# Gathers of a graph network's edge stage read their indices in place

## What is computed

```python
def _L1_gnn_ref(h, rbf, edge_index, We1, be1, We2, be2, Wlin, Wn1, bn1, Wn2, bn2):
    src, dst = (edge_index[0], edge_index[1])
    w = silu(rbf @ We1 + be1) @ We2 + be2          # per edge, 200000 x 64 -> 128
    m = w * (h[src] @ Wlin)                        # row of the source node
    agg = segment_sum(m, dst, num_segments=h.shape[0])
    out = silu(agg @ Wn1 + bn1) @ Wn2 + bn2
    return h + out
```

## Time and profile before

| | |
|---|---|
| median of 3 runs | 4196.25 us (4185.68 to 4204.25) |
| profiled execution | 4190.64 us, span 4188.9 us |
| PE busy | 3078.5 us (73%) |
| DVE busy | 2098.1 us (50%) |
| POOL busy | 1449.0 us (35%), nearly all in the edge stage |
| ACT busy | 962.0 us (23%) |
| DMA | 325.5 MB, mean 78 GB/s; q1 (hardware queues) 15.9% of the DMA engines' time, q0 (GpSimd's) 8.9% |

### The profile page before, as it was taken

One profiled execution on the slowest core, in us unless ns is written; L12 is line 12 of the kernel. 1 busy time (PEld: TensorE's weight loads), 2 busy tenths in 40 slices (PEclk: granted clock), 3 DMA queues, 4 the chain that ended last, 5 costly groups with the idle time before them and its releaser, 6 DMA issues.

```text
span 4188.9 us, 82895 instructions
## 1 busy us (share of the span) xinstructions
PE 3078.5 (73%) x19882; PEld 2243.1 (54%) x19883; DVE 2098.1 (50%) x4806; ACT 962.0 (23%) x2058; POOL 1449.0 (35%) x1549
## 2 busy tenths in 40 slices
PE   6979999999979966666666666666666666666667
PEld 5623567777769954444444444444444444444445
DVE  8999999999984432333223332233322333323333
ACT  4101244566641111111111111111111111111111
POOL 0000000000000034555555555555555555555552
PEclk8989999999999977777777777777777777777778
DMA  1000111222237932222222222222222222222222
GB/s 52 0 0 32 47 78 78 109 109 109 109 155 298 344 121 57 59 57 59 59 60 59 57 59 60 60 59 57 59 60 60 59 59 58 59 60 59 57 57 58
DMA packets 289446, 325.50 MB, mean 78 GB/s; under 512 B 236303, under 2 KB 249640, under 8 KB 276606
## 3 DMA queue, kind: packets, MB, share of 16 engines
q1 hardware_dynamic: 234382, 218.90, 15.9%
q0 software_dynamic: 49504, 102.66, 8.9%
q10 hardware_dynamic: 5264, 1.36, 0.1%
HBM read 237.69 MB, written 85.09 MB: 77 GB/s over the span
## 4 chain that ended last, share of the span: by engine, by line
PE 40%; ACTq 26%; issue 25%; DVE 4%; ACT 3%; DVEq 1%; another core or an unknown queue 1%; DMA 0%; SPq 0%; POOL 0%; POOLq 0%
ACTq L390 20%; PE pa L1543 8%; PE pb L1395 7%; PE pa L1395 7%; PE pc L1389 5%; ACTq L386 5%; PE pd L1389 4%; PE pd L1353 2%; ACT shared L786 2%; PE pb L1554 1%; PE pf L1355 1%; PE pc L1571 1%; PE pb L1480 1%; DVE shared L1030 1%
## 5 line engine op out<-in xcount | busy, mean ns | idle before, releaser
L544 POOL DMA_INDIRECT shared<-lin_table,idx x1516 | 1434.1, 946 | 1183.0 <-ACT idx L666 542.3
L1543 PE MATMUL pa<-shared,we_sb 64*128 64x512 f32 x784 | 393.8, 1096 | 945.2 <-ACT shared L786 835.5
L1543 PEld LDWEIGHTS pa<-shared,we_sb 64*128 64x128 f32 x784 | 95.8, 296 | 984.8 <-ACT shared L786 869.4
L573 POOL DMA_DIRECT2D lin_table<-c x12 | 9.3, 772 | 1498.6 <-issue 1308.9
L1225 DVE TENSOR_TENSOR agg<-agg,pf 128x128 f32 x98 | 28.3, 289 | 891.0 <-remote 868.8
L1554 PE MATMUL pb<-we_sb,shared 128*128 128x128 f32 x3136 | 460.1, 290 | 6.6 <-issue 6.6
L1225 DVE TENSOR_TENSOR agg<-agg,pc 128x128 f32 x98 | 28.3, 289 | 855.5 <-remote 806.0
L1554 PEld LDWEIGHTS pb<-we_sb,shared 128*128 128x128 f32 x3136 | 384.5, 193 | 96.5 <-issue 96.0
L666 ACT ACTIVATE idx<-idx_all 128x8 int32 (+1 forms) x196 | 40.8, 210 | 1683.3 <-issue 1683.3
L1030 DVE TENSOR_SCALAR shared<-col_h,shared 128x784 bf16<-128x784 f16 x1092 | 408.9, 426 | 5.1 <-issue 4.3
L791 ACT ACTIVATE shared<-pa,be_col 128x512 f32<-128x512 f32 x392 | 248.3, 685 | 483.5 <-PE pa L1543 344.8
(11 more groups left out here) (238 smaller groups left out, 4286.9 us busy)
## 6 DMA issues: line engine op xcount, KB each, us to landing
adjacency<-shared SPq DMA_DIRECT2D x49, 1568.0 KB, 5.6
shared<-adjacency SPq DMA_DIRECT2D x49, 1568.0 KB, 8.7
table_sb<-lin_table SPq DMA_DIRECT2D x3384, 0.5 KB
shared<-in_edge_attr_dram SPq DMA_DIRECT2D x195, 256.0 KB
table_sb<-lin_table ACTq DMA_DIRECT2D x2632, 0.5 KB
shared<-lin_table,idx POOLq DMA_INDIRECT x1516
lin_table<-c POOLq DMA_DIRECT2D x12, 256.0 KB, 7.1
out_dram<-xr SPq DMA_DIRECT2D x12, 256.0 KB
```

The lines of the kernel that those rows point to most:

```text
L544: pool.indirect_dma_start(out=dest(s, j), out_offset=None, in_=table, in_offset=bass.IndirectOffsetOnAxis(ap=idx[:, s, j:j + 1], axis=0)). ...
L1543: pe.matmul(pa[:, h, :], we1_sb[half, :], ea_t[half, :], start=True, stop=True).then_inc(hid_mm, 1)
```

## The change

GpSimd's gathers in the edge stage take each tile's row numbers from its column of `idx_all` in place of the block `idx[s]`. The column's place is a constant in each instruction, so GpSimd's loop over turns is written out turn by turn. GpSimd no longer waits for `idx_ready` in this stage, and ScalarE no longer copies index blocks for it nor waits for landed gathers. The wait for `msg_ready` stays as it was. The two passes that are taken only when a test at run time asks for them keep `gather`, `idx` and the copies.

```diff
-            def linear_rows(s, j):
-                return gat[:, s, j, :]
+            def linear_gather(g, s, tiles=U):
+                for j in range(tiles):
+                    pool.indirect_dma_start(
+                        out=gat[:, s, j, :], out_offset=None, in_=lin_table,
+                        in_offset=bass.IndirectOffsetOnAxis(ap=idx_all[:, g * U + j:g * U + j + 1], axis=0)).then_inc(lin.gathered[s], 16)
 
             def gather_turn(it, tiles):
                 for s in range(RING):
-                    pool.wait_ge(lin.idx_ready, it * RING + (s + 1))
                     pool.wait_ge(msg_ready, (it * RING + (s - RING + 1)) * 2)
                     pool.sem_inc(passed, 1)
-                    gather(lin, lin_table, linear_rows, s, tiles if s == RING - 1 else U)
+                    linear_gather(it * RING + s, s, tiles if s == RING - 1 else U)
             for s in range(RING):
-                pool.wait_ge(lin.idx_ready, s + 1)
-                gather(lin, lin_table, linear_rows, s)
-            with pool.Fori(1, ITERS - 1) as it:
+                linear_gather(s, s)
+            for it in range(1, ITERS - 1):
                 gather_turn(it, ASIDE)
             gather_turn(ITERS - 1, LAST_TILES)
...
-            first_idx(lin)
             edge_act(0)
...
             def act_turn(it, par=None):
                 for s in range(RING):
                     edge_act(it * RING + (s + 1), None if par is None else (it + 1, par, s))
-                    after_gather(lin, it, s, 1 if s == RING - 1 else 0)
```

## The result

The changed kernel takes 4323.4 us, median of its five runs, against 4196.25 us. Two of the five lie near 4565 us and the others near 4320 us, and it is with the latter that the ratio is 1.029 (95% interval 1.027 to 1.031), slower. The profile read here is from a second set of runs of the same kernel (x1_after_again: execution 4325.2 us, span 4323.5 us, against a span of 4188.9 us before). The two spans differ by 134.6 us. The gather stands in a function of its own now, L582 for L544, and the code behind it has moved by a line: the sums' addition L1224 for L1225, the products L1207 and L1203 for L1208 and L1204, ScalarE's activation after a batch L787 for L786.

A forecast was written before the change was run, and what follows sets the result against it. The bound was taken as a loop through GpSimd, whose batches hold TensorE's results. 4190.6 us plus +0.93 us x 190 = +177 us, other terms taken as nothing, gave 4368 us; range 4150 to 4530 us.

The forecast's parts named there:

- from then on every batch needs the products that VectorE makes in this very gap: Edge stage: without the index wait, VectorE's products gate GpSimd's batches; +177 us, chance 0.60.
- hardly ever holds it now: GpSimd's msg_ready wait before a batch: seldom binding in the kernel before, since its products were made the previous turn.
- The early one: Gap between GpSimd's batches when VectorE already had its sums: 4.12 us, +0.08 us a batch, +15 us in all.
- a short gap gives less time and the next is long: Gaps between GpSimd's batches: short and long both occur, so the middle was taken, 4.97 us.
- The index copies: ScalarE's copies and wait for gathered: 32 us if ScalarE alone set the pace, nothing where products set the gap.
- The operand: GpSimd's gathers reading the table with longer rows: taken as 0, bounded by -0.01 to +0.08 us a gather.
- The loop written out: GpSimd's 47 turns written in a line: taken as 0, with 123 us either way as the bound.
- ScalarE's last row issue: Sign in the edge stage: it would come sooner after a batch's end than 2.3 us.
- (a): Rival: GpSimd runs pairs of batches end to end, -125 us, 4066 us; chance 0.14.
- (b): Rival: ScalarE's queue is the bound, so only its 0.17 us a group go, 4159 us; chance 0.12.
- (c): Rival: GpSimd without gaps starves ScalarE's row issues, +400 us, 4590 us; chance 0.09.
- that it ends with the batch is: TensorE's results reach VectorE only some 2 us after GpSimd's batch has ended, whether 8 or 7 gathers.

The follow-up runs named there:

- experiment 2: Changed kernel with GpSimd's wait for ScalarE's idx_ready signal put back, nothing copied; 4170.4 us, ratio 0.990 to the kernel before.
- experiment 9: Changed kernel with row transfers split evenly, 16 issues a group each on SyncE and ScalarE; 4239.7 us, ratio 1.020 to the kernel before.
- experiment 3: Kernel before with GpSimd's loop over turns written out and nothing else; 4194.6 us, ratio 0.997.
- experiment 5: Changed kernel with all eight tiles gathered by GpSimd and no row issues on ScalarE and SyncE; 4155.0 us, ratio 0.987 to the kernel before.
- experiment 4: Changed kernel with GpSimd also waiting for the second layer's matmuls of the group three before; 4297.9 us, ratio 1.021 to the kernel before.
- experiment 6: Changed kernel with four gathers a group, their rows used twice in the products; 3875.1 us, ratio 0.921 to the kernel before.
- experiment 7: Kernel of experiment 2 with one row transfer a group moved from ScalarE to SyncE (19 and 13 issues); 4432.2 us, ratio 1.053 to the kernel before.
- experiment 8: Kernel of experiment 4 with two row transfers a group moved from SyncE to ScalarE (16 and 16); 4065.1 us, ratio 0.965 to the kernel before.

## Why the prediction was right, and where it wasn't

**Direction and mechanism: right.** The step "from then on every batch needs the products that VectorE makes in this very gap" is in the waits: 175 gaps put down to L1207 and L1203, where before the index copy ended most. Experiment 2 settles it: the same gathers, the same indices, the wait back, and the loss is gone. Span and gaps agree (134.6 against 135 us). The 0.80 us from products to gather, which came from one place, holds: it is 0.80 or 0.81 us in all 165 gaps put down to products between 1700 and 4060 us.

This also settles what looked like a weak point. The prediction said that msg_ready "hardly ever holds it now", while the earlier trace rows puts 224.0 us of the gaps before down to L1208. In 49 of the 50 such gaps between 1700 and 4060 us the last product ended only 0.04 to 0.60 us before the gather, too late to have released it. One is in the earlier trace rows: the gather starts at 2536.78, before the products' end at 2537.33, and the index copy stands as far ahead of it as in the first of these gaps (0.88 and 0.89 us):

```profile
2535.69 0.21 ACT L666 ACTIVATE idx<-idx_all 128x8 int32 x1 [8.54 <-issue]
```

**The size: +135 us for the +177 forecast; the early end was mis-sized.** I took the middle of two gaps, 5.82 and 4.12 us. The late one measures 5.93 us, near the sum of rows that gave it. The early one measures 3.50 us, not 4.12: I had it from one place of the trace before, where the products ended 3.32 us after the batch, and in the changed kernel they end as little as 2.4 us after a batch of 7 gathers, where half of them is made while the batch still runs. With 3.50 the middle is 4.71 us, +0.67 us, +128 us. So the even mixture, which I had argued as "a short gap gives less time and the next is long", held almost exactly: 94 and 90, and the two kinds take turns. That it came out even is in part luck. The prediction's reason, the length of the gap before, doesn't force it: in experiment 9 the gaps are ended by products as well, and there short ones follow short ones. The sum also had no term for the split of the rows, on which 0.9 of the 2.9% hang.

**The index copies: right in size.** Forecast -32 us where they count, together with ScalarE's wait for landed gathers. They count nothing in the changed kernel, whose gaps end with products; where ScalarE's signal ends the gap (experiment 2 against 3) they bring some 28 us.

**The operand: nothing, as forecast.** The gathers' minimum, median and maximum are those of the earlier trace rows to the nanosecond.

**The loop written out: forecast 0, measured 0.3% faster.** The Trainium skill (Advanced Engine Details and Errata, ISA Cache) gives the size of the instruction cache, but no price of a refill and no word on loops; the estimate of +20 us for refills was worked out from it with a row of ScalarE. The runs don't bear the estimate out: experiment 3 is some 12 us faster, and the steps between gathers are the same 0.30 us.

**ScalarE's last row issue: not sooner than 2.3 us, but sooner than before.** The 2.3 us were those of one batch. The rows below give 2537.91, 2552.72 and 2566.45, which is 3.69, 2.55 and 2.49 us after the ends at 2534.22, 2550.17 and 2563.96. These are late ones: over the batches of 1700 to 4060 us the median is 2.36 us, against 2.64 us in the kernel before.

```profile
2530.69 7.22 ACTq L390 DMA_DIRECT2D table_sb<-lin_table  x14
...
2544.48 8.24 ACTq L390 DMA_DIRECT2D table_sb<-lin_table  x14
...
2557.47 8.98 ACTq L390 DMA_DIRECT2D table_sb<-lin_table  x14
```

So the sign as it was worded wasn't met, and the step behind it, that ScalarE's issues end sooner after a batch in a longer turn, holds weakly, by some 0.3 us. The chain that ended last still gives ScalarE's queue 26%, yet no gap is put down to it; whether the changed kernel would gain from fewer issues on ScalarE was not tried.

**The rivals.** (a), pairs of batches, appears in the changed kernel only at the stage's two ends; it appears in experiment 5, where no rows are issued, as the forecast's reason against it said, and there gives 13.4 us a group rather than 12.8. (b), ScalarE's queue as the only bound, fell: it would have made the changed kernel as fast as experiment 2. (c), ScalarE's issues starved, didn't come, but its likeness did in another place that I hadn't weighed: SyncE. In experiments 4, 6 and 7 it is SyncE's 18 or 19 issues that come too late: its queue has 40, 43 and 33% of their chains. The prediction read ScalarE's queue because the chain named it and left out the other one, which had 0% of the chain and almost no slack.

**What stays open.** That GpSimd's gathers hold TensorE's results is shown, since the hold-up ends earlier when the run of gathers is cut to half and stays when the row issues are gone; by what means they hold them isn't. Nor is the rule by which some get out: in the changed kernel the dividing line lies near 4.5 us into a batch (the latest that wasn't held was finished at 4.56 us, the earliest that was at 4.35 us), but in experiment 6 results finished 3.0 to 4.0 us into a batch were held while some finished at 3.3 to 3.5 us were not, and in experiment 9 seven in ten get out before the end (126 of 175 between 1700 and 4100 us), many after the sixth gather. The prediction's "that it ends with the batch is" (in the profile) holds in the changed kernel and nearly always in experiments 5 and 6. It fails in experiment 9, and it wasn't quite so in the kernel before either: there 13 of 140 sums finished during a batch of 8 got out 1.8 to 4.7 us later and yet before its end. The part of the split in the changed kernel's loss is known by experiment 9 alone, as 0.9% across two chips; a changed kernel with fewer rows on both engines was not run.

## What to carry to other kernels

When a wait is taken out, the next wait in line sets the release; find when that comes, from the trace, and whether the old wait kept the engine a step behind its buffers, so that the next one was always met. The moment of release can be worth more than the work: here a wait without any work, put where the second layer ends, together with an even split of row issues, gave 3.5%, and either alone was slower than the kernel before. And a queue that has 0% of the chain may have no slack: move one issue onto it and see, before something else is made faster.

## What the runs showed of the chip

A run of GpSimd's gathers mostly holds back TensorE's finished results from VectorE until after its last gather: by 1.3 us after a run of 4 (experiment 6), 2.0 us after 8 (the changed kernel) and 3.3 us after 16 (experiment 5, where the median wait is 14.9 us with no row transfers issued beside them; after its rarer runs of 8 the median is 3.5 us). In the changed kernel results that TensorE finishes early in a run aren't held (2544.94, added at 2545.08), and in experiment 9 most get out before its end.

Row issues on ScalarE and SyncE go more slowly beside those gathers. In the changed kernel (x1_after_again, pauses over 2.5 us left out) SyncE starts one every 0.70 us on average while a batch runs and every 0.37 us in the gaps, ScalarE every 0.56 and 0.44 us. In the three turns above 14 issues of ScalarE take 7.2 to 9.0 us; in experiment 8 SyncE's 16 take 11.1 us and ScalarE's 8.7 us:

```profile
2540.79 11.07 SPq L390 DMA_DIRECT2D table_sb<-lin_table  x16
2544.00 8.73 ACTq L390 DMA_DIRECT2D table_sb<-lin_table  x16
```

The Trainium skill (DMA: Bandwidth & Descriptors, Issuing engines are not separate DMA queues) says that spreading transfers over engines saves only the time to initiate them, which it calls usually small beside the transfer. Here that time bounds the stage in experiments 4 and 7, and one issue a group moved between the two engines changed the kernel's time by 6% (experiments 2 and 7).
